# Another order for the first four slots of an attention and sampling pipeline: guess, halves, casts

## The reference, cut to what matters

```python
# x: 64 batches x 64 tokens x 512; 16 heads of 32
xn = rms_norm(x, g_norm) * (1 + scale) + shift       # scale, shift = cond @ W_emb + b_emb
q, k, v = heads(xn @ W_qkv)
q, k = rms_norm(q, g_q), rms_norm(k, g_k)            # per head: needs rsqrt of a mean of squares
attn = softmax(q @ k.T / sqrt(32))                   # "P" below
o = attn @ v
x = x + o + o @ W_out
ix = (cond + 1) / 2 * 511                            # "grid": cond is the grid of layer 2; indices clipped
x = x + (1 - w) * x[floor(ix)] + w * x[floor(ix)+1]  # per batch, taps along the features
x = x + GRU(x); x = x + oscillators(x)               # uses tanh(q) @ coupling.T
```

## Time and profile before

| | us |
|---|---|
| median of 3 runs | 1549.43 (1543.22, 1551.79, 1549.43) |
| profiled execution | 1551.52 |
| its span | 1549.7 |
| TensorE busy | 1492.9 (96%) |
| VectorE busy | 1393.2 (90%) |
| ScalarE busy | 946.1 (61%) |
| GpSimd busy | 759.6 (49%) |

### The profile page before, as it was taken

The page is one execution under the profiler, slowest core; times in us unless marked ns, Lnnn a source line. Parts: engine busy times, 40 slices in busy tenths (PEclk is TensorE's granted clock), DMA queues, the critical chain, the costliest instruction groups (busy, mean ns, idle before and its releaser), DMA issues.

```text
span 1549.7 us, 95828 instructions
## 1 busy us (share of the span) xinstructions
PE 1492.9 (96%) x42219; PEld 1321.8 (85%) x42219; DVE 1393.2 (90%) x3291; ACT 946.1 (61%) x2884; POOL 759.6 (49%) x949
## 2 busy tenths in 40 slices
PE   6899999999999998899999999999999999999995
PEld 4577766677766668899999999999999999999994
DVE  7899999999999988598998999888889988988987
ACT  6677777777777763455555555555555555555553
POOL 2567677766667755434433433334343434333331
PEclk9999999999999999999999999999999999999998
DMA  6333433344443342000000000000000000000000
GB/s 228 61 91 87 91 95 88 87 99 110 103 110 103 81 110 76 4 15 14 12 15 15 14 13 15 15 15 12 15 15 13 14 15 14 13 14 15 14 13 16
DMA packets 170019, 75.60 MB, mean 49 GB/s; under 512 B 140729, under 2 KB 155233, under 8 KB 169601
## 3 DMA queue, kind: packets, MB, share of 16 engines
q1 hardware_dynamic: 169504, 69.44, 19.4%
q10 hardware_dynamic: 96, 0.02, 0.0%
HBM read 33.71 MB, written 11.60 MB: 29 GB/s over the span
## 4 chain that ended last, share of the span: by engine, by line
PE 89%; DVE 5%; issue 2%; ACT 1%; POOL 1%; ACTq 0%; POOLq 0%; DVEq 0%
PE psB L1489 35%; PE psA L1518 15%; PE psQ L1180 13%; PE psA L1523 8%; PE psQ L1222 7%; PE psO L1270 5%; PE psB L1204 2%; PE psA L1158 2%; DVE room L804 1%; PE psO L1258 1%; PE psB L1279 1%; DVE ss L826 1%; ACT front L519 1%; DVE oT L893 1%; POOL S L435 0%
## 5 line engine op out<-in xcount | busy, mean ns | idle before, releaser
L1489 PE MATMUL psB<-first,Wx 128*128 128x64 f16 x9216 | 292.7, 193 | 5.8 <-POOL first L1801 3.8
L1518 PE MATMUL psA<-ts,Cp 128*128 128x64 f16 x8160 | 283.3, 193 | 12.0 <-ACT ts L1556 10.9
L1489 PE MATMUL psB<-first,Whh 128*128 128x64 f16 x9072 | 286.9, 193 | 0.9
L1489 PEld LDWEIGHTS psB<-first,Wx 128*128 128x128 f16 x9216 | 279.7, 98 | 7.2 <-POOL first L1801 3.9
L1489 PEld LDWEIGHTS psB<-first,Whh 128*128 128x128 f16 x9072 | 273.9, 98 | 2.0 <-issue 1.8
L1556 ACT ACTIVATE ts<-qst 128x256 f16<-128x256 f32 x192 | 80.1, 417 | 314.6 <-DVE qst L1660 314.6
L1180 PE MATMUL psQ<-Wx,front 128*128 128x512 f16 x1152 | 267.3, 382 | 3.9 <-DVE front L982 3.9
L1518 PEld LDWEIGHTS psA<-ts,Cp 128*128 128x128 f16 x8160 | 257.6, 98 | 14.0 <-ACT ts L1556 11.8
L1180 PEld LDWEIGHTS psQ<-Wx,front 128*128 128x128 f16 x1152 | 108.3, 98 | 122.2 <-DVE front L982 4.2
L804 DVE TENSOR_SCALAR room<-rows,lidx 128x512 f16<-128x512 f16 x256 | 182.2, 754 | 0.2
L1797 POOL TENSOR_TENSOR en<-rz,dn 128x256 f32<-128x256 f32 x64 | 46.6, 729 | 257.9 <-issue 257.7
(11 more groups left out here) (201 smaller groups left out, 3015.6 us busy)
## 6 DMA issues: line engine op xcount, KB each, us to landing
front<-in_x SPq DMA_DIRECT2D x32, 256.0 KB, 2.9
rows<-rows_dram SPq DMA_DIRECT2D x64, 128.0 KB, 2.9
out<-ot SPq DMA_DIRECT2D x512, 16.0 KB, 1.8
x<-x SPq DMA_DIRECT2D x29, 224.0 KB
Whh<-in_L_cond_W_qkv SPq DMA_DIRECT2D x12, 256.0 KB, 8.0
room<-in_L_cond_W_hh SPq DMA_DIRECT2D x12, 256.0 KB, 2.8
room<-in_L_cond_W_ih SPq DMA_DIRECT2D x12, 256.0 KB, 2.7
wih_dram<-room SPq DMA_DIRECT2D x12, 256.0 KB, 3.0
```

The lines of the kernel that those rows point to most:

```text
L1489: last = mm(o, W_[:, i, c, g * PART:(g + 1) * PART], src[:, j, c, :], start=False, stop=False, skip_group_check=True)
L1518: mm(psF[:, s % 2, m, :], Cp[:, i, c, m * PART:(m + 1) * PART], ts_[:, 0, c, :], start=(c == 0 and m == 0 and i == 0), stop=False, skip_gr ...
```

## The change

It has five parts, all of them in the first four slots. (1) ScalarE, slot 0: `guess(2)`, the first roots of q and k of pair 0 and of x of pair 2, stands ahead of `high_x(1)` and `high_cp(0)`. (2) VectorE, slot 1: `grid_middle` stands behind `low_qk(0)`. (3) VectorE, slot 1: `low_cp(1)` stands ahead of `least(0)`. (4) ScalarE: the `high_halves` of pairs 0 and 1 move from the end of the slot of their scores to the next slot, behind `high_qk`. (5) GpSimd: their `low_halves` move to the next slot too, behind `modulate`.

```diff
--- before.py
+++ after.py
@@ -467,6 +467,8 @@ (gpsimd, slot)
             if p := pair(1):
                 modulate(p)
+            if (p := pair(-2)) and p.n < 2:
+                low_halves(p)
             if i == 2:
                 low_wo(KC - 1)
@@ -482,7 +484,7 @@
             if p := pair(-1):
                 norm_p(p)
-                if p.n <= N2.n:
+                if 1 < p.n <= N2.n:
                     low_halves(p)
@@ -658,6 +660,9 @@ (scalar, slot)
                 high_qk(p, 0)
                 high_qk(p, 1)
+            if (p := pair(-2)) and p.n < 2:
+                high_halves(p, 0)
+                high_halves(p, 1)
             if i == 0:
                 squares_qk(pair(0), 0)
@@ -674,6 +679,8 @@
             if i == 2:
                 high_wo(KC - 1)
+            if i == 0:
+                guess(2, QK_X)
             if p := pair(1):
                 high_x(p)
@@ -688,7 +695,8 @@
                 high_o(p)
-            guess(i + 2, QK_X if pair(2) else QK)
+            if i > 0:
+                guess(i + 2, QK_X if pair(2) else QK)
@@ -702,9 +710,7 @@
-            if p := pair(-1):
-                if p.n < 2:
-                    high_halves(p, 0)
+            if (p := pair(-1)) and p.n > 1:
                 high_halves(p, 1)
@@ -1004,13 +1010,13 @@ (vector, slot)
                 scale_x(p)
-            if i == 1:
-                grid_middle()
             if tap and tap.n > 0:
                 build(tap, 0, (0,))
             if p := pair(-1):
                 low_qk(p, 0)
                 low_qk(p, 1)
+            if i == 1:
+                grid_middle()
@@ -1022,12 +1028,12 @@
             if i == 3:
                 weights_of_taps()
+            if i == 1:
+                low_cp(1)
             if p := pair(-1):
                 least(p)
                 if p.n < 2:
                     subtract_least(p)
-            if i == 1:
-                low_cp(1)
             sums_qk(qk, 1)
```

## The result

The changed kernel takes 1554.81 us in the median (1552.66 to 1558.76), the kernel before 1548.93 on the same chip: ratio 1.0044, 95% interval 1.0032 to 1.0057, which is 6.8 us more (5.0 to 8.8); the two medians themselves differ by 5.9. Timed again on another chip, in four executions, the ratio was 1.0071 (1.0045 to 1.0097), which is 11 us (7 to 15). The profiled execution took 1554.93, its span is 1553.1. Busy times of the whole are nearly unchanged (TensorE 1493.1, VectorE 1393.7), but that total hides something.

What follows compares the result with a forecast made beforehand. TensorE, gapless from slot 4 until the recurrences, was taken as the bound. Roots -1.3, low halves +5.85, projection -0.4, slot 3 +1.2 and clock +2.2 gave +7.5 us, 1557 from a median of 1549.43; range 1547 to 1562.

Steps and rivals of the forecast that it cites:

- the class: Whole kernel against a 0.5% bound (7.7 us): same 0.54, slower 0.43, faster 0.03.
- Roots, -1.3 forecast: Slots 0 and 1: Ln 0.9 us earlier, Newton steps shorter, qn 1.5 us sooner, norm_p(0)'s end about 1.3 us sooner.
- Low halves of pair 0, +5.85 behind `norm_p`: Slot 2, GpSimd: three W_out pieces (3.7 us) and the modulation (2.15) go first; first mix 4.5 us later, at 62.0.
- rival (B): First mix: same wait but cheaper, transposes landing in 3.3 us or the clock staying up; 1553.3 to 1555.5, chance 0.23.
- P's high halves: Slot 2: scores of pair 1 start near 50.5 instead of 53.11, 2.6 us gained only if what follows is ready.
- Projection, -0.4: Slot 2: the 0.39 us wait before pair 0's projection goes, since high_o no longer comes late behind high_x(3).
- Clock in slot 2, +2.2: TensorE idle 7.8 us before the first mix, then matmuls at half clock: 2.2 us, lower bound 0.
- Slot 3, +1.2 forecast: Pair 1's low halves stand behind modulate(4): second mix 10.2 us into the slot instead of 9.0, costing 1.2 us.
- The carry to the end: From slot 4 until the recurrences TensorE has no gap, so earlier gains or losses carry on one for one.
- Rival (D): Slot 2: GpSimd reaches the low halves in time, mix starts at 54.2, gain 3.7 us, 1545.7; chance 0.06.
- Rival (C): Worse: half clock at 2.9 us and slot 3's transposes landing slowly (+1.5), 9.7 us in all, 1559; chance 0.21.

Runs made afterwards that it cites:

- part 1's kernel: Only guess(2) moved ahead of high_x(1) and high_cp(0), against the kernel before; ratio to before 0.9979 (0.9965 to 0.9993).
- the kernel with the filling: Changed kernel plus 26 and 11 idle matmuls on TensorE while it waits for the first and second transposes; ratio to before 1.0019 (1.0000 to 1.0038).
- parts 1 to 4: Changed kernel with the low halves of pairs 0 and 1 put back right behind norm_p; ratio to before 0.9985 (0.9966 to 1.0004).
- only pair 0 late: Changed kernel with pair 1's low halves back behind norm_p(1), pair 0's still late; traced once without a ratio, slot 4 at 90.4 us.
- the two second traces: Kernel before and changed kernel each traced again, unaltered; slot 4 at 84.8 and 92.1 us, the changed one's ratio 1.0071 (1.0045 to 1.0097).
- the mended kernel: Kernel before with parts 1 to 3, pair 0's high halves late, W_out's three low pieces behind modulate(3); ratio to before 0.9985 (0.9971 to 0.9999).

## Why the prediction was right, point by point

The sign and the mechanism were right (+6.8 measured, +7.5 forecast): the low halves behind five instructions, TensorE standing still for them, the clock behind that. That the total came so close is in part luck, since errors of -1.5 and +2.6 us in two terms offset each other. So is the class, "same" within 0.5%: the forecast lay 0.2 us inside that bound, and on the second chip the change measured 0.71%.

- **Roots, -1.3 forecast, -1.0 measured.** Against the start of slot 0 (18.83, before 18.66) `qn` starts 1.3 us sooner and `norm_p(0)` 1.0. The two ingredients were right, in the lines of the earlier trace rows:

```profile
...
29.30 0.23 ACT L521 ACTIVATE lm<-ms 128x33 f32<-128x33 f32 x1
...
29.83 0.20 DVE L824 TENSOR_TENSOR rt<-rs 128x33 f32<-128x33 f32 x1 [0.56 <-ACT rs L521]
...
30.52 1.29 DVE L839 TENSOR_TENSOR qn<-psQ,rs 128x512 f32<-128x512 f32 x2
...
34.98 1.15 DVE L940 CAST x<-um 64x512 int32<-64x512 f32 x1
...
36.16 0.42 DVE L942 CAST x<-x 64x512 f32<-64x512 int32 x1
```

Ln at 29.30, directly behind the means, and a first Newton step of 0.20 (before 0.39). That the step is short only while GpSimd rests agrees in its direction with what the Trainium skill says of the shared port pair (SBUF — State Buffer, "SBUF: two separate sides"). No run shows a lock for a whole instruction: in the earlier trace rows the step starts at 30.43 and `low_x` ends at 30.77, so waiting for that end and then 0.20 us would make 0.54, and it took 0.39. In this kernel it is the first cast (L940) that now meets the modulation, 1.15 us against 0.41 in part 1's kernel, where the second one does. Together with the 0.2 us that `low_qk(0)` waits, parts 2 and 3 give back 0.3.
- **Low halves of pair 0, +5.85 behind `norm_p`.** Measured: from `norm_p`'s end at 49.35 to 55.16, 5.8 us. But the first mix came 3.5 us later and not 4.5, and TensorE stood still for 6.3 us and not 7.8: the transposes landed in 3.2 us and not in the 4.7 of the earlier trace rows. This is the piece of my rival (B) that came true. My reading, that the first transposes are slow because they are the first, has fallen. The slower of the two landed in 4.6 to 5.1 us in all eight traces that issue them before 52 us, in 3.3 to 3.4 in the five that issue them later, but in 4.6 in the kernel with the filling, which issues them at 56.8; pair 1's took up to 4.7 and 4.9 in two others (parts 1 to 4; only pair 0 late). What makes them slow stays open. No run measured it by itself.
- **P's high halves.** The scores of pair 1 started 2.05 us sooner, forecast 2.6, and as forecast nothing of it was gained, since the mix was not ready.
- **Projection, -0.4.** The wait is gone, as expected.
- **Clock in slot 2, +2.2.** 1.72 + 4.23 against 1.19 + 2.76: +2.0, shown by the filling.
- **Slot 3, +1.2 forecast, +3.8 measured.** The step that was mis-sized. The second mix was 11.05 us into the slot, not 10.2:

```profile
...
71.49 0.69 DVE L794 TENSOR_TENSOR front<-psB,rsB 128x512 f32<-128x512 f32 x1
...
72.26 1.05 POOL L457 TENSOR_TENSOR front<-front,modA 128x512 f32<-128x512 f32 x1 [2.76 <-DVE front L794]
...
73.38 1.22 POOL L457 TENSOR_TENSOR front<-front,modB 128x512 f32<-128x512 f32 x1
...
74.56 2.37 POOL L441 TENSOR_TENSOR front<-S,front 128x512 f16<-128x512 f32 x2
...
75.79 3.35 SPq L317 DMA_TRANSPOSE PT<-front  x2
```

`scale_x` (L794) ends 2.2 us into the slot as worked out; then the modulation takes 2.3 instead of 2.15, and the two transposing DMAs take 3.35 us to issue instead of 2.73, the second starting 2.1 us behind the first and not 1.4. The slow issue is of this place and not of one execution: 3.2 to 3.45 us in all six traces with pair 1's low halves late, 2.6 in the eight others; why stays open. And the clock fell a second time, which I had priced in slot 2 alone: +1.7. It fell in three of the five traces with a wait of 2.6 to 2.9 us at this place, so it is a matter of the execution.
- **The sum.** On the span's own clock the roots bring 0.8 (48.14 to 47.31): -0.8 + 5.8 - 1.5 (landing) - 0.4 + 2.0 + 3.8 = +8.9, against 8.7 read at slot 4. The carry to the end was right: between 86 and 560 us the changed kernel has the same single wait of 0.4 us as the earlier trace rows, and the first output step comes 9.8 us later (670.5 against 660.7; in the two second traces 7.0 us). The spans of the profiled executions differ by 3.4 us only, since the recurrences of the changed one happened to take 6.4 us less; the timings, over ten executions each, say 6.8.

Rival (D), the hidden low halves, is excluded by the 6.31 us wait. Rival (C) had the right place, slot 3, with its price there for another reason: the transposes of pair 1 landed in 3.1 to 3.6 us, and it was their issue and the clock that cost.

## What to carry to other kernels

When an instruction is moved a stage later on an in-order engine, count everything in the list between its old and its new place, and follow it to the first engine that waits: here five instructions of 5.8 us on an engine that is 49% busy held up the one that is 96% busy. A wait of a few microseconds on TensorE costs more than its length, because the matmuls behind it may run at half speed: 2.0 and 1.7 us more here, behind 6.31 and 2.67 us. And in a kernel whose later part varies by 6 us from one execution to the next, read the position at the end of the changed stage, not the total.

## What the runs showed of the hardware that I had not expected

- The granted clock fell to 0.50 behind quite short waits. In the mended kernel 1.01 us and 1.36 us of waiting in slot 2 were followed by a projection at 1.2 GHz (4.34 us instead of 2.76); in the changed kernel's second trace 1.48 and 0.28 us (1.79 and 3.78 instead of 1.09 and 2.75). The first trace of that kernel had the same two waits and kept 2.4 GHz (1.09 and 2.75). In slot 3 it was the other way round: 4.45 us in the first trace and 2.76 in the second, behind waits of 2.67 and 2.64.
- Two transposing DMAs on one queue, unchanged in size, landed anywhere from 3.1 to 5.1 us after issue.
- The 64 steps of the recurrences, the same instructions in each kernel, mostly take 14.0 us each, with spells of 14.2 to 15.1 that come at other steps in each execution.
